# A decoder layer on one core: one sum of magnitudes for two weight pieces, a plain copy of the total, and scaled scores written back to PSUM

## The chip, the core and the metric

The kernel runs on one core of one Trainium2 chip. The core has five engines with queues of their own: TensorE (PE, matrix multiply; PEld is its weight load), VectorE (DVE), ScalarE (ACT), GpSimd (POOL) and SyncE (SP, which here only issues transfers). They meet through semaphores. Matrix products are written to PSUM (eight banks of 128 partitions x 512 fp32 values), everything else lives in SBUF. The metric is the device time of one execution in microseconds, lower is better.

## What is computed

A decoder layer with three residual blocks, each followed by a layer norm: self attention with 16 heads of 128 on x of 2 x 512 x 512, whose weights are 4-bit codes times a scale per 32 rows; cross attention against a memory of 2 x 1024 rows with only the 54 largest scores of a row kept; and a gated feed-forward block.

```python
w = codes * jnp.repeat(scales, 32, axis=0)            # for q, k, v and o
scores = einsum('bqhd,bkhd->bhqk', q, k) / sqrt(128)
attn = softmax(scores, axis=-1)
out = einsum('bhqk,bkhd->bqhd', attn, v)              # then o, residual, layer norm
# cross attention: scores, keep the 54 largest of 1024, softmax, product, W_o, residual, layer norm
# feed forward: silu(x Wg) * (x Wu), then Wd, residual, layer norm
```

The change touches the self attention alone.

## The kernel before, in words

To keep fp32 accuracy on TensorE, every operand is split into a high half (rounded to the format that TensorE reads, written by ACT) and a low half (the remainder, written by DVE or POOL), and a product is the sum of three matmuls: low x high, high x high, high x low. For the four weights the low half is often all zero, since a 4-bit code times a power of two is exact in the high half. The kernel finds that out at run time. For each weight key (a head pair of q and k, a group of v, a pair of o) it sums the magnitudes of the low half, and if the sum is 0 it skips the matmuls with the low half by a branch in `mm_if` (line 105).

That sum is made of these steps. When the low half of a piece (128 x 512) has been written, `check_lo` (line 225) notes it. `run_checks` (line 228) stands near the end of each step of the main loop and takes up to two noted pieces from the list, each with one ACT instruction `Abs` with an accumulated sum into a column of `mag` (line 235). The hardware runs that as two instructions, the ACTIVATE and an ACTIVATION_READ_ACCUMULATOR. A q/k key (18 of them) has two pieces, w = 0 for q and w = 1 for k; an o key (8) has two pieces; a v key (4) has four. When the last piece of a key is summed, `run_sums` (line 241) in the next step adds the 128 partitions with one small matmul against `ones` (line 247), and ACT adds the two or four columns with a copy that accumulates into `flag` (line 250). TensorE's queue later loads the flag (line 109).

The main loop (line 1099) runs over 128 steps i = 4 j + qt, where j is a pair of head and batch and qt a quarter of the rows. Each step puts on the queues, for TensorE in this order: projections of the next j (`proj_qk`, qt 0 and 1), at qt 3 the transposes of step i, at qt 0 the product with V (`av`), at qt 2 and 3 the output projection (`proj_o`), in some j the V projection (`proj_v`), else the transposes, then `scores(i + 2)` (three matmuls), and from `run_sums` the sum of magnitudes. `scores` (line 494) also puts on DVE a multiply by minus the scale with a running minimum (line 503), whose full output goes to a scrap tile `JK` in bf16 and whose minimum goes to `nms`. `softexp(i + 2)` (line 507) is the exponential on ACT, which reads the raw scores in PSUM again, multiplies by the scale `ssc` (one value per partition, from SBUF) for heads above 1 and a constant for heads 0 and 1. All queues are first in, first out, in the order in which the program's steps are written; within a step ACT gets evacuations (L370, L396, L438, L535, L554), the exponential, then the checks, then high halves of new weight pieces (L277). DVE gets the minimum (L503) ahead of the low halves of q/k (L373) and of the transposed probabilities (L538). `run_sums` does nothing at qt = 0.

Where a v key's last piece is noted (step 3 of the j with j % 8 = 5), the first piece of a q/k key is noted in the same step, so `run_checks` takes both in the step after.

Of the kernel before, what the change touches and what calls it, by code (L numbers as in the profile page):

```python
# [63 lines left out]
def decoder_layer(nc, xT, xn, wq, sq, wk, sk, wv, sv, wo, so, bqk, bv, bo,  # L64
                  xwq, xwo, ctxT, ctxn, scal, wg, wu, wd, rq, rk, out):
    with ExitStack() as top:
# [81 lines left out]
        mag = sbt(top, "mag", [128, 4, 4])  # L148
        fsum = sbt(top, "fsum", [1, 4])
        flag = sbt(top, "flag", [1, 32])  # L150
        ssc = sbt(top, "ssc", [128, 2])
        JA = sbt(top, "JA", [128, 512], BF16)
# [27 lines left out]
        JK = sbt(ph1, "JK", [128, 512], BF16)  # L180
# [42 lines left out]
        FL = {}  # L223

        def check_lo(key, lo, tl):
            checks.append((now[0], key, lo, tl))

        def run_checks():
            for _ in range(2):
                if not checks or checks[0][0] >= now[0]:  # L230
                    return
                _, key, lo, tl = checks.pop(0)
                n, col, ts = FL.setdefault(key, (4 if key[0] == "v" else 2, len(FL), []))
                m = mag[:, col % 4, len(ts):len(ts) + 1]
                T[("JA",)] = op(act, lambda e, lo=lo, m=m: e.activation(JA[:, :], lo, ACT.Abs, accum_out=m),  # L235
                                tl, T.get(("JA",)), T.get(("flag", col - 4)))
                ts.append(T[("JA",)])
                if len(ts) == n:
                    sums.append((now[0], key))

        def run_sums():
            while sums and sums[0][0] < now[0]:
                _, key = sums.pop(0)
                n, col, ts = FL[key]
                k, ps = fbank()
                o = ps[0:1, 0:n]
                t = pe.add(lambda e, o=o, col=col, n=n: e.matmul(o, ones[:, 0:1], mag[:, col % 4, 0:n],  # L247
                                                                 start=True, stop=True),
                           flat([ts, t_one, bank[5 + k]]), True)
                t = op(act, lambda e, o=o, col=col, n=n: e.activation(fsum[:, 0:n], o, ACT.Copy,  # L250
                                                                       accum_out=flag[:, col:col + 1]),
                       t, T.get(("flag", col - 1)))
                bank[5 + k] = T[("flag", col)] = t

        def flag_of(key):
            c = FL[key][1]
# [237 lines left out]
        def scores(i):  # L494
# [8 lines left out]
            tm = op(dve, lambda e: e.tensor_scalar(JK[:, :], ps, nsc, None, ALU.mult, ALU.min, accum_out=m),  # L503
# [942 lines left out]
```

How the kernel before makes its waits and increments, by code:

```python
    def emit(self, eng):  # L38
        reached = {}
        for waits, fn, inc in self.items:
            for sem, v in waits:
                if reached.get(id(sem), 0) < v:
                    reached[id(sem)] = v
                    eng.wait_ge(sem, v)
            if fn is None:
                continue
            ins = fn(eng)
            if inc:
                ins.then_inc(self.sem, 1)
# [33 lines left out]
            def load(self, dst, src, *waits, q=sp):  # L83
                self.n += 1
                s = self.sem
                q.add(lambda e: e.dma_start(dst, src).then_inc(s, 16), flat(waits), False)
                return (s, 16 * self.n)
```

## Time and profile before

| what | value |
|---|---|
| median of 3 runs | 970.77 us (970.51 to 971.89) |
| the profiled execution's own time | 969.9 us |
| its span in the trace | 968.0 us |
| instructions in the trace | 13301 |
| TensorE matmul busy | 928.5 us (96%) |
| ACT busy, DVE busy, POOL busy | 580.8, 577.3, 473.7 us |
| self attention (the main loop) | about 27 to 545 us of the span |

Times in the rows are microseconds from the start of the span. "Busy" of TensorE counts a matmul of 512 columns as about 0.39 us, though such matmuls start every 0.23 us when nothing holds them, so a busy TensorE can hide short holes. Where a row ends in brackets, they give the engine's idle time before it and the instruction whose end released it. Self attention, in which all that the change touches lies, is the first 545 us.

### The profile page before, as it was taken

What the parts mean: (1) busy time and instruction counts of PE and PEld (TensorE: products, weight loads), DVE (VectorE), ACT (ScalarE), POOL (GpSimd) and SP (SyncE); (2) the same over time, 40 slices, a digit from 0 to 9 for tenths busy, and PEclk for the clock granted to TensorE, in tenths of its full rate; (3) what the DMA queues carried; (4) which work ended last, traced back from release to release, by engine and by line L of the source; (5) the groups of instructions that cost most, each with busy time, mean ns of one, the idle gap of its engine ahead of it and who ended that gap; (6) DMA issues with size and microseconds to landing.
All of it is one profiled execution on the core that took longest, in us unless ns stands there. A gap on an engine that the chain in (4) does not pass through costs nothing.

```text
span 968.0 us, 13301 instructions
## 1 busy us (share of the span) xinstructions
PE 928.5 (96%) x4516; PEld 751.6 (78%) x4516; DVE 577.3 (60%) x1057; ACT 580.8 (60%) x1201; POOL 473.7 (49%) x375
## 2 busy tenths in 40 slices
PE   9999899999999999999999999899999899999997
PEld 7777678877788777877667777788878788788886
DVE  5676756567566666565675799884878314511114
ACT  5667866678767778687775446443564634443333
POOL 4246642545515356466554347452684652354440
PEclk9999999999999999999999999989999999999999
DMA  6531220212300222222222112331443341243331
GB/s 197 153 109 44 85 85 1 62 54 71 87 12 28 88 58 68 66 60 72 50 66 87 55 55 88 88 98 50 126 110 98 89 141 43 76 134 97 99 87 43
DMA packets 46101, 76.97 MB, mean 80 GB/s; under 512 B 5584, under 2 KB 11216, under 8 KB 45776
## 3 DMA queue, kind: packets, MB, share of 16 engines
q1 hardware_dynamic: 45600, 75.68, 26.8%
q8 instruction: 41, 0.67, 0.3%
q10 hardware_dynamic: 432, 0.39, 0.1%
q14 instruction: 28, 0.23, 0.1%
HBM read 73.69 MB, written 2.36 MB: 79 GB/s over the span
## 4 chain that ended last, share of the span: by engine, by line
PE 81%; DVE 9%; ACT 5%; issue 3%; DMA 1%; POOL 0%; SPq 0%; DVEq 0%; ACTq 0%; POOLq 0%
PE p L99 75%; PE p L528 5%; DVE JK L503 2%; DVE acc L447 1%; ACT PR L511 1%; ACT JA L235 1%; DVE PT L538 1%; DVE QK L373 1%; DMA acc<-in_xT 1%; DVE m L726 1%; PE p L779 1%; DVE st L588 0%; PE p L636 0%; DVE SX L737 0%; PE p L247 0%
## 5 line engine op out<-in xcount | busy, mean ns | idle before, releaser
L503 DVE TENSOR_SCALAR_CACHE_REDUCE JK<-p,ssc 128x512 bf16<-128x512 f32 x112 | 83.8, 748 | 149.5 <-PE p L99 149.1
L654 POOL TENSOR_TENSOR V<-RAW,V 128x512 fp32r<-128x512 f32 x64 | 82.6, 1311 | 141.8 <-ACT V L653 141.7
L444 POOL TENSOR_TENSOR acc<-SX,acc 128x512 f32<-128x512 f32 x52 | 68.7, 1320 | 169.8 <-ACT SX L438 131.4
L99 PE MATMUL p<-R 128*128 128x512 f32 x544 | 136.8, 394 | 2.0 <-DVE V L399 0.8
L99 PE MATMUL p<-QK 128*128 128x512 f32 x384 | 117.4, 414 | 4.5 <-DVE QK L373 4.1
L511 ACT ACTIVATE PR<-p,nms,ssc 128x512 f32<-128x512 f32 x112 | 87.2, 778 | 57.5 <-DVE JK L503 57.1
L99 PEld LDWEIGHTS p<-R 128*128 128x128 f32 x544 | 100.9, 188 | 26.5 <-issue 1.4
L99 PE MATMUL p<-R,V 128*128 128x512 f32 x480 | 113.4, 392 | 0.8 <-ACT C L653 0.8
L99 PEld LDWEIGHTS p<-R,V 128*128 128x128 f32 x480 | 90.6, 189 | 20.1 <-issue 1.2
L275 POOL TENSOR_TENSOR RAW<-RAW,SCL 128x512 f32<-128x512 f32 x65 | 87.4, 1350 | 27.0 <-DMA SCL<-in_so 14.3
L654 POOL TENSOR_TENSOR C<-RAW,C 128x512 fp32r<-128x512 f32 x58 | 75.9, 1322 | 41.1 <-ACT C L653 41.1
L99 PE MATMUL p<-PT,V 128*128 128x512 f32 x384 | 93.6, 393 | 1.9 <-DVE PT L538 1.9
L99 PE MATMUL p<-C 128*128 128x512 f32 x384 | 92.5, 390 | 0.2 <-issue 0.2
L99 PE MATMUL p<-WV,R 128*128 128x512 f32 x368 | 91.0, 394 | 1.3 <-DVE JK L503 1.1
L99 PE MATMUL p<-V 128*128 128x512 f32 (+1 forms) x432 | 90.8, 367 | 0.7 <-POOL V L654 0.7
L887 DVE TENSOR_TENSOR SX<-p,SX 128x512 f32<-128x512 f32 x32 | 22.1, 691 | 115.0 <-PE p L99 108.9
L538 DVE TENSOR_TENSOR PT<-p,PT 128x512 fp32r<-128x512 f32 x128 | 87.4, 683 | 5.0 <-ACT PT L535 4.9
L99 PEld LDWEIGHTS p<-PT,V 128*128 128x128 f32 x384 | 70.6, 188 | 20.4 <-issue 2.5
L99 PEld LDWEIGHTS p<-V 128*128 128x128 f32 x432 | 74.5, 189 | 14.1 <-ACT V L653 1.1
L99 PEld LDWEIGHTS p<-C 128*128 128x128 f32 x384 | 71.7, 188 | 15.2 <-issue 0.6
L99 PEld LDWEIGHTS p<-WV,R 128*128 128x128 f32 x368 | 67.8, 188 | 18.7 <-issue 3.0
L99 PE MATMUL p<-WO,OT 128*128 128x512 f32 x256 | 74.7, 412 | 3.2 <-DVE acc L447 2.7
(170 smaller groups left out, 1665.8 us busy)
## 6 DMA issues: line engine op xcount, KB each, us to landing
RAW<-in_wg SPq DMA_DIRECT2D x32, 256.0 KB, 2.8
RAW<-in_wu SPq DMA_DIRECT2D x32, 256.0 KB, 2.7
RAW<-in_ctxn SPq DMA_DIRECT2D x32, 256.0 KB, 2.8
RAW<-in_wd SPq DMA_DIRECT2D x32, 256.0 KB, 2.8
RAW<-in_wq SPq DMA_DIRECT2D x19, 256.0 KB, 2.7
RAW<-in_wk SPq DMA_DIRECT2D x18, 256.0 KB, 2.7
RAW<-in_wv SPq DMA_DIRECT2D x16, 256.0 KB, 2.8
RAW<-in_wo SPq DMA_DIRECT2D x16, 256.0 KB, 4.4
```

Source lines behind the costliest of these rows:

```text
L99: return e.matmul(outp, a, b, start=st, stop=sp_)
L235: T[("JA",)] = op(act, lambda e, lo=lo, m=m: e.activation(JA[:, :], lo, ACT.Abs, accum_out=m), tl, T.get(("JA",)), T.get(("flag", col - 4)))
L275: tm = op(em, lambda e: e.tensor_tensor(rv, rv, sv_, ALU.mult), td, ts)
L373: tl = op(dve, lambda e: e.scalar_tensor_tensor(out=lo, in0=ps, scalar=bias, in1=hi, op0=ALU.add, op1=ALU.subtract), th, free, T_BQK)
L444: pool, lambda e: e.tensor_tensor(a, buf, a, ALU.add), ts, T[("acc", r)])
L447: bank[5 + k] = T[("scaled", j)] = T[("acc", r)] = op(dve, lambda e: e.scalar_tensor_tensor(out=a, in0=ps, scalar=s, in1=a, op0=ALU.mult, ...
L503: tm = op(dve, lambda e: e.tensor_scalar(JK[:, :], ps, nsc, None, ALU.mult, ALU.min, accum_out=m), T[("S", i)], T.get(("max", i - 1)), T.g ...
L511: T[("exp", i)] = op(act, lambda e: e.activation(PR[:, i % 2, :], ps, ACT.Exp, bias=m, scale=sc, accum_out=rs[:, i % 8:i % 8 + 1]), T[("ma ...
L528: t = pe.add(lambda e, c=c: e.transpose(tp[:, c], PR[:, i % 2, c], ident[:, :]), flat([T[("exp", i)], free, t_id]) if kt == 0 else [], kt ...
L538: tl = op(dve, lambda e: e.tensor_tensor(lo, tv, hi, ALU.subtract), th, fr)
L654: tl = op(pool, lambda e: e.tensor_tensor(lo, raw, hi, ALU.subtract), th, free)
L887: t = op(dve, lambda e: e.tensor_tensor(hf, u, hf, ALU.mult), T[("g", n, 1)], t)
```

## The change

It has three parts.

1. `check_lo` now collects the pieces of a key and notes the key once, when its last piece is written. `run_checks` takes one key in a step and sums two pieces (128 x 2 x 512) with one `Abs`: one instruction for a q/k or o key, two for a v key. In all 34 `Abs` of 1024 elements stand in for 68 of 512.
2. `run_sums` adds the partials of a v key in PSUM (two small matmuls that accumulate), so that one value is left, and ACT writes it to `flag` with a plain copy. The tile `fsum` and the wait for the flag before go.
3. The minimum on DVE writes the scaled scores over the raw ones in PSUM (fp32, 128 x 512) instead of a scrap tile in SBUF (bf16), and the exponential reads them with the constant factor -1 instead of the scale from SBUF. The wait of a minimum for the minimum before goes.

```diff
-        mag = sbt(top, "mag", [128, 4, 4])
-        fsum = sbt(top, "fsum", [1, 4])
+        mag = sbt(top, "mag", [128, 4, 2])
-        JA = sbt(top, "JA", [128, 512], BF16)
+        JA = sbt(top, "JA", [128, 2, 512], BF16)
-        JK = sbt(ph1, "JK", [128, 512], BF16)
...
         def check_lo(key, lo, tl):
-            checks.append((now[0], key, lo, tl))
+            n, ts = PIECES.setdefault(key, (4 if key[0] == "v" else 2, []))
+            ts.append(tl)
+            if len(ts) == n:
+                checks.append((now[0], key, list(ts)))
...
         def run_checks():
-            for _ in range(2):
-                if not checks or checks[0][0] >= now[0]:
-                    return
-                _, key, lo, tl = checks.pop(0)
-                n, col, ts = FL.setdefault(key, (4 if key[0] == "v" else 2, len(FL), []))
-                m = mag[:, col % 4, len(ts):len(ts) + 1]
-                T[("JA",)] = op(act, lambda e, lo=lo, m=m: e.activation(JA[:, :], lo, ACT.Abs, accum_out=m),
-                                tl, T.get(("JA",)), T.get(("flag", col - 4)))
-                ts.append(T[("JA",)])
-                if len(ts) == n:
-                    sums.append((now[0], key))
+            if not checks or checks[0][0] >= now[0]:
+                return
+            _, key, ts = checks.pop(0)
+            col = FL.setdefault(key, len(FL))
+            lo = low_halves(key)
+            done = []
+            for n in range(0, lo.shape[1], 2):
+                m = mag[:, col % 4, n // 2:n // 2 + 1]
+                T[("JA",)] = op(act, lambda e, m=m, n=n: e.activation(JA[:, :, :], lo[:, n:n + 2, :], ACT.Abs, accum_out=m),
+                                ts, T.get(("JA",)), T.get(("flag", col - 4)))
+                done.append(T[("JA",)])
+            sums.append((now[0], key, done))

         def run_sums():
...
-                t = pe.add(lambda e, o=o, col=col, n=n: e.matmul(o, ones[:, 0:1], mag[:, col % 4, 0:n],
-                                                                 start=True, stop=True),
-                           flat([ts, t_one, bank[5 + k]]), True)
-                t = op(act, lambda e, o=o, col=col, n=n: e.activation(fsum[:, 0:n], o, ACT.Copy,
-                                                                       accum_out=flag[:, col:col + 1]),
-                       t, T.get(("flag", col - 1)))
+                for n in range(len(ts)):
+                    t = pe.add(lambda e, ps=ps, col=col, n=n: e.matmul(
+                        ps[0:1, 0:1], ones[:, 0:1], mag[:, col % 4, n:n + 1], start=n == 0, stop=n == len(ts) - 1),
+                        flat([ts, t_one, bank[5 + k]]), n == len(ts) - 1)
+                t = op(act, lambda e, ps=ps, col=col: e.activation(flag[:, col:col + 1], ps[0:1, 0:1], ACT.Copy), t)
...
-            tm = op(dve, lambda e: e.tensor_scalar(JK[:, :], ps, nsc, None, ALU.mult, ALU.min, accum_out=m),
-                    T[("S", i)], T.get(("max", i - 1)), T.get(("exp", i - 4)))
+            tm = op(dve, lambda e: e.tensor_scalar(ps, ps, nsc, None, ALU.mult, ALU.min, accum_out=m),
+                    T[("S", i)], T.get(("exp", i - 4)))
...
-            sc = ssc[:, 0:1] if HB[i // 4][0] > 1 else SC
...
-                PR[:, i % 2, :], ps, ACT.Exp, bias=m, scale=sc, accum_out=rs[:, i % 8:i % 8 + 1]),
+                PR[:, i % 2, :], ps, ACT.Exp, bias=m, scale=-1.0, accum_out=rs[:, i % 8:i % 8 + 1]),
```

## Rows read from the trace of the kernel before

**Rows 1.** The page: busy us, share of the span, instructions, by engine
```profile
PE 928.5 (96%) x4516; PEld 751.6 (78%) x4516; DVE 577.3 (60%) x1057; ACT 580.8 (60%) x1201; POOL 473.7 (49%) x375
```

**Rows 2.** Three stretches: length, busy PE, PEld, DVE, ACT, POOL, TensorE clock, DMA, GB/s
```profile
0.00:545.00 545.00, 528.88 (x2560) 416.40 (x2561) 344.34 (x696) 384.95 (x875) 267.29 (x215) 1.00 0.24 71
...
618.00:628.60 10.60, 7.07 (x35) 5.38 (x33) 8.82 (x16) 4.26 (x8) 2.56 (x2) 1.00 0.18 53
...
628.70:638.90 10.20, 7.40 (x33) 7.03 (x34) 10.13 (x19) 7.70 (x15) 8.24 (x7) 0.50 0.27 77
```

**Rows 3.** Groups by line and shape: busy us, mean ns of one, idle before
```profile
L511 ACT ACTIVATE PR<-p,nms,ssc 128x512 f32<-128x512 f32 x112 | 87.2, 778 | 57.5 <-DVE JK L503 57.1
L503 DVE TENSOR_SCALAR_CACHE_REDUCE JK<-p,ssc 128x512 bf16<-128x512 f32 x112 | 83.8, 748 | 149.5 <-PE p L99 149.1
...
L235 ACT ACTIVATE JA<-R 128x512 bf16<-128x512 f32 x36 | 22.3, 619 | 0.3
...
L602 DVE TENSOR_SCALAR acc<-acc,mv,rstd 128x512 f32<-128x512 f32 x20 | 12.6, 675 | 0.2
...
L511 ACT ACTIVATE PR<-p,nms 128x512 f32<-128x512 f32 x16 | 11.0, 688 | 9.3 <-DVE JK L503 9.3
...
L235 ACT ACTIVATION_READ_ACCUMULATOR JA<-R 128x1 f32 x36 | 6.8, 189 | 0.0
...
L734 ACT ACTIVATE SCL<-SX,nmx 128x1024 f32<-128x1024 f32 x4 | 4.6, 1152 | 0.0
...
L924 DVE TENSOR_TENSOR acc<-p,acc 128x512 f32<-128x512 f32 x4 | 2.7, 680 | 1.1 <-PE p L99 1.1
```

**Rows 4.** Who waited for whom: us in total, times, longest
```profile
PEld p L247 <- ACT JA L235: 8.5, 14, 1.4
...
PE p L99 <- DVE QK L373: 4.4, 15, 0.9
PE p L247 <- ACT JA L235: 3.3, 4, 1.0
```

**Rows 5.** Timeline of a step with a q/k sum: start, length, engine, line
```profile
196.29 0.78 ACT L511 ACTIVATE PR<-p,nms,ssc 128x512 f32<-128x512 f32 x1 [0.42 <-DVE JK L503]
...
197.06 0.62 ACT L235 ACTIVATE JA<-R 128x512 bf16<-128x512 f32 x1
197.06 0.93 PE L99 MATMUL p<-QK 128*128 128x512 f32 x3 [0.25 <-DVE QK L373]
...
197.58 0.19 ACT L235 ACTIVATION_READ_ACCUMULATOR JA<-R 128x1 f32 x1
...
197.93 0.19 PE L247 MATMUL p<-mag,ones 128*1 128x2 f32 x2
```

**Rows 6.** Timeline of a step with a v sum
```profile
249.89 0.62 ACT L235 ACTIVATE JA<-WV 128x512 bf16<-128x512 f32 x1
...
250.41 0.19 ACT L235 ACTIVATION_READ_ACCUMULATOR JA<-WV 128x1 f32 x1
250.69 0.63 ACT L235 ACTIVATE JA<-R 128x512 bf16<-128x512 f32 x1
...
251.20 0.19 PE L247 MATMUL p<-mag,ones 128*1 128x4 f32 x2
```

**Rows 7.** Timeline of the steps around an o sum
```profile
238.10 0.62 ACT L235 ACTIVATE JA<-WO 128x512 bf16<-128x512 f32 x1
...
239.79 0.08 DVE L503 DVE_READ_ACCUMULATOR JK<-p,ssc 128x1 f32 x1
...
240.28 0.78 ACT L511 ACTIVATE PR<-p,nms,ssc 128x512 f32<-128x512 f32 x1
...
241.56 0.21 ACT L235 ACTIVATION_READ_ACCUMULATOR JA<-WO 128x1 f32 x1
...
241.86 0.19 PE L247 MATMUL p<-mag,ones 128*1 128x2 f32 x2 [0.78 <-ACT JA L235]
...
242.24 0.47 PE L99 MATMUL p<-R 128*128 128x512 f32 x1 [0.19 <-issue]
```

More of the change, by code:

```diff
@@ L222, in decoder_layer @@
         checks, sums = [], []
-        FL = {}
+        FL, PIECES = {}, {}
         def check_lo(key, lo, tl):
-            checks.append((now[0], key, lo, tl))
-        def run_checks():
-            for _ in range(2):
-                if not checks or checks[0][0] >= now[0]:
-                    return
-                _, key, lo, tl = checks.pop(0)
-                n, col, ts = FL.setdefault(key, (4 if key[0] == "v" else 2, len(FL), []))
-                m = mag[:, col % 4, len(ts):len(ts) + 1]
-                T[("JA",)] = op(act, lambda e, lo=lo, m=m: e.activation(JA[:, :], lo, ACT.Abs, accum_out=m),
-                                tl, T.get(("JA",)), T.get(("flag", col - 4)))
-                ts.append(T[("JA",)])
-                if len(ts) == n:
-                    sums.append((now[0], key))
+            n, ts = PIECES.setdefault(key, (4 if key[0] == "v" else 2, []))
+            ts.append(tl)
+            if len(ts) == n:
+                checks.append((now[0], key, list(ts)))
@@ new lines, in low_halves @@
+        def low_halves(key):
+            if key[0] == "v":
+                return WV[:, 1, :, :]
+            if key[0] == "o":
+                return WO[:, key[1] % 2, :, 1, :]
+            return WQK[:, key[1] % 2, :, 1].rearrange("p w k c -> p w (k c)")
+        def run_checks():
+            if not checks or checks[0][0] >= now[0]:
[10 more added lines that the diff above has]
+            sums.append((now[0], key, done))
@@ L241, in run_sums @@
         def run_sums():
             while sums and sums[0][0] < now[0]:
-                _, key = sums.pop(0)
-                n, col, ts = FL[key]
+                _, key, ts = sums.pop(0)
+                col = FL[key]
                 k, ps = fbank()
-                o = ps[0:1, 0:n]
-                t = pe.add(lambda e, o=o, col=col, n=n: e.matmul(o, ones[:, 0:1], mag[:, col % 4, 0:n],
-                                                                 start=True, stop=True),
-                           flat([ts, t_one, bank[5 + k]]), True)
@@ L253, in run_sums @@
+                t = op(act, lambda e, ps=ps, col=col: e.activation(flag[:, col:col + 1], ps[0:1, 0:1], ACT.Copy), t)
                 bank[5 + k] = T[("flag", col)] = t
         def flag_of(key):
-            c = FL[key][1]
+            c = FL[key]
             return flag[0:1, c:c + 1].bitcast(I32), T[("flag", c)]
```

## The prediction, made before the result

> **What bounds the kernel now.** I read the page first. TensorE is busy 96% of the span, ACT and DVE 60% each [rows 1]. Over the first 545 us, where all of the change lies, TensorE is busy 528.9 us at the full clock and ACT 385.0 us, that is 71% [rows 2]. So TensorE sets the time, and 16 us of open holes are left in this stage. Work taken off ACT or DVE counts only where TensorE waits for exactly that work, and work that comes later counts in full where TensorE waits for it. The table of waits says who it waits for. The longest entry by far is the small matmul of the sum of magnitudes (L247) waiting for ACT's `Abs`: 8.5 us at the weight load and 3.3 us at the matmul, 18 times. The next is the first scores of a new j, which wait for the low half of q/k on DVE, 15 times, 4.4 us [rows 4]. The change moves both places. It takes instructions off ACT and makes the last one before each sum longer. The third view is the timeline around the 30 sums, for the slack between the end of the accumulator read and the sum on TensorE. There are four kinds:
>
> - **Tight q/k sums.** At 197.93 the sum starts 0.16 us after the read ends at 197.58 + 0.19 [rows 5]. Ten sums look like this one: at 72.6, 86.3, 197.9, 211.5, 322.4, 335.9, 447.8, 461.4, 477.4 and 492.0 us, the first two with a slack of 0.25.
> - **Sums that stall already.** At 241.86 TensorE stood idle 0.78 us and started 0.09 us after the read's end at 241.56 + 0.21 [rows 7]. So 0.09 is the gap when the sum waits for the read. Four of these, all for o, at 117.4, 241.9, 366.4 and 464.8.
> - **v sums** with four columns. At 251.20 the v read ended at 250.60, 0.60 us before [rows 6]. Three of these, at 126.7, 251.2 and 375.7. The first v sum at 35.2 is apart.
> - The other twelve have 0.7 to 2.9 us of slack.
>
> **The long `Abs`.** The trace has no `Abs` of 1024. A 128x512 takes 619 ns, and the read behind it 189. An exponential of 1024 takes 1152 with a bias from SBUF; a factor from SBUF costs ACT 778 - 688 = 90 ns in L511 [rows 3]. Taking 90 off for the bias gives 1.06 us, so the second half costs 0.43 us (1.06 - 0.62). Bounds: 0.37 (1.152 against the dearest exponential of 512, 0.778) and 0.53 (1.152 - 0.619, nothing taken off). An `Abs` of 512 takes 0.80 from start to start [rows 6], so one of 1024 takes 1.23. ACT loses 34 x (0.80 - 0.43) = 13 us of work, the 30 accumulator reads after the flag copy another 5.6 us at 0.19, and 112 exponentials 90 ns each, 10 us [rows 3]. That is 28 us of ACT in all, and it lies beside TensorE's work except as follows.
>
> **What it does to each kind.** A q/k key's two `Abs` ran in two consecutive steps, right behind the exponential. Now the first is gone and the second is 0.43 longer, and the sum is still in the step behind. The exponential before it starts when DVE's minimum is done (it waits 0.42 us for it [rows 5]), so taking the first `Abs` away does not start it earlier. Only its own 0.09 is gained. The read ends 0.34 later, of which 0.07 is slack (0.16 - 0.09), so the sum waits 0.27 us and TensorE with it. I count nine of the ten (2.4 us); the one at 461.4 is followed 3.4 us later by a stalled o sum that takes it up.
>
> For the stalled o sums the first `Abs`, at 238.10, is removed, and ACT runs without a pause from there to the exponential at 240.28. That one can come earlier until the minimum, which ended at 239.87, holds it: by some 0.36. With its own 0.09 the `Abs` starts 0.45 earlier and lasts 0.43 longer [rows 7]. Four times nothing.
>
> A v key's four `Abs` were spread over four steps, and only the last, with a q/k `Abs` behind it, stood before the sum. Now both long ones do. The first starts at 249.80, the second 1.23 later at 251.03, its read starts 0.95 on (0.52 plus 0.43) and ends at 252.17; with 0.09 the sum starts at 252.26 instead of 251.20, 1.06 later [rows 6]. Three times, 3.2 us. ACT's next evacuations move by about the same, no more than TensorE does. The q/k `Abs` moves to the step behind, where its sum had 2.8 us of slack. The first v sum: both long `Abs` now run in a stretch where ACT waits until 30 us anyway, and a plain copy brings the flag some 0.1 us sooner, which is waited for: -0.1.
>
> Where a sum stalls, TensorE's queue has drained, and what its sequencer does next is exposed. After the stalled sum the next matmul starts 0.38 us on (242.24), after the sum at 197.93 another starts 0.12 on [rows 5, 7]. The difference is the load of a flag, which follows each v sum too: 3 x 0.26 = 0.8 us. A tight q/k sum is followed by transposes with no load: 0, at most 9 x 0.26 = 2.3. The extra small matmul of a v key adds 0.03 us.
>
> **The scores written back.** DVE writes no PSUM in this trace. Its operations of 512 elements that differ in where they read take 675 ns (SBUF) and 680 (PSUM), and the largest step between forms of the minimum is 748 against that 675, 73 ns [rows 3]. I take 0 for the price, with bounds of -30 and +75 ns. The minimum stands on the path at the first scores of a new j, 15 times, since DVE's low half is queued behind it [rows 4], and at some ten places late in the stage; so -0.7 to +1.9 us. The dropped wait for the minimum before is on the same queue and long met. The constant factor is worth 90 ns of the exponential, already counted.
>
> The Trainium skill (Perfetto Trace Analysis, Optimizing Scalar/DVE Operations) gives DVE about 60 ns per access on SBUF and 125 on PSUM. By that the minimum would take 65 ns more and the sum 1.6 us more; the rows of reads do not show such a difference.
>
> **The sum.** 2.4 + 3.2 + 0.8 - 0.1 = +6.3 us on the profiled execution's 969.9, so 976.2. The median of the runs lies 0.9 above that execution, so 977.1 us.
>
> **The rivals.**
>
> - **Faster: the relief of ACT removes the stalls.** If ACT is generally late rather than at the last `Abs`, 28 us less work pulls the exponential and the read ahead, the four stalled o sums lose their 0.78 and 0.26 us, and half of the 4.4 us at first scores goes too. 970.8 - 4.2 - 2.2 = 964.4 us. For it: the exponential at 240.28 was late by 0.36 us. Against: in [rows 5] it waited for DVE. It decides from the point where an `Abs` of 1024 costs under 0.1 us more than one of 512. Chance 0.15. The same page and section says that larger operations improve throughput "if the engine is saturated", and that where ACT causes bubbles on others though it isn't, "breaking up instructions may allow work to be completed sooner". ACT at 71% with TensorE waiting for it is that second case, which agrees with my forecast.
> - **No change: what the sums lose is given back.** Later waits of TensorE on DVE could shrink when TensorE comes later. They are waits behind a minimum that itself follows TensorE's scores, so I give it little: 970.8 + 0.8 = 971.6 us, chance 0.15.
> - **Slower still: the write to PSUM is slow.** If DVE paid a second pass over the elements (0.53 us, as the 512 elements take), 25 places would cost 13 us: 990 us, chance 0.05. If it only pays the 75 ns and sequencer time is exposed at each q/k sum, 977.1 + 1.9 + 2.3 = 981.3, which is inside my range.
> - **The clock.** TensorE ran at half clock (1.2 of 2.4 GHz) from 628.7 to 638.9 us, after a stretch of 10.6 us in which it was busy for 7.1 [rows 2]. The change moves this by 6 us. If the slow stretch fell away, at most 5 us come back (972); if such a one were added, 982. Chance 0.1 in all, one half each.
> - **The change does not do what it says** on the factor: if the constant -1 gained nothing, each sum would wait 0.09 longer, 1.1 us in all. The 16 exponentials with a constant speak against it [rows 3]. It stays in the range.
>
> **How the numbers follow.** The forecast of 977.1 has 0.55, with a range of its own of 974 to 981 (the long `Abs` at 0.37 to 0.53 acts once in nine sums and twice in three, so -0.9 and +1.5, DVE by -0.7 and +1.9). A range of 80% reaches over the clock's and the no-change case down to 970, and up to 981.5. A measurement of this kernel can tell about 0.2% (1.9 us) from no change. Faster by more: 0.15. Within 0.2%: the no-change case and a little of the rest, 0.17. Slower: 0.68.
>
> **What would show it.** `Abs` x34 at 1.04 to 1.06 us. The wait of L247 for ACT's `Abs` grows from 11.8 us to 17 or more and from 18 times to over 28. The ten tight sums show a gap of 0.09 instead of 0.16, the v sums start about 1.1 us later behind their scores. The minimum stays near 748 ns, the exponential falls to 688. I would be wrong if the waits at L247 shrink, if the minimum's row moves by more than 75 ns, or if the waits for L373 change by more than 2 us.

## The result and the profile after

The changed kernel takes 977.83 us (median of 4 runs, 977.24 to 978.35), the kernel before 970.64 (4 runs, 969.92 to 971.89). The ratio is 1.0068 with an interval of 1.0057 to 1.0080, so the change costs 7 us. The forecast was 977.1.

| what | before | after |
|---|---|---|
| profiled execution, its span | 969.9, 968.0 us | 977.64, 975.8 us |
| instructions in the trace | 13301 | 13072 |
| ACT busy | 580.8 us | 562.9 us |
| TensorE waits for ACT's `Abs` at the sum (at the weight load + at the matmul; the two overlap in time) | 8.5 + 3.3 us | 15.6 + 8.0 us |
| main loop, first transpose of `PR` to last | 512.2 us | 519.2 us |

The last row is the measure that the rest of this text uses. The loop's start differs by 1.4 us between two profiles of the changed kernel (31.6 and 30.2), and the stages behind the loop, which no edit touches, take 425.0 to 428.2 us in the thirteen profiles of this text. So one span says little about an edit of 1 us, and the loop more. It is read from the view of one tile: operation, lengths, start of the first and of the last. Before:

```profile
L528 PE MATMUL p<-ident,PR x512: 270/272/330, 30.0 to 542.2; 128*128 128x128 f32 x171
```

After:

```profile
L534 PE MATMUL p<-ident,PR x512: 270/272/330, 31.6 to 550.8; 128*128 128x128 f32 x171
```

The loop is 7.0 us longer with 18 us less work on ACT. The engines' line of the page after answers to [rows 1]:

```profile
PE 930.0 (95%) x4524; PEld 751.1 (77%) x4524; DVE 578.6 (59%) x1057; ACT 562.9 (58%) x1103; POOL 473.1 (48%) x375
```

Two stretches of after, with the columns of [rows 2]: the self attention, and the 10 us in which TensorE is granted half its clock, which came 7 us later with everything else.

```profile
0.00:553.60 553.60, 531.79 (x2568) 416.76 (x2569) 346.03 (x696) 367.17 (x777) 267.05 (x215) 1.00 0.24 70
...
635.80:646.00 10.20, 6.05 (x28) 5.69 (x29) 10.09 (x20) 8.36 (x15) 6.90 (x6) 0.51 0.23 60
```

The groups by line and shape, against [rows 3]:

```profile
L517 ACT ACTIVATE PR<-p,nms 128x512 f32<-128x512 f32 x128 | 87.8, 686 | 80.6 <-DVE p L510 80.4
L510 DVE TENSOR_SCALAR_CACHE_REDUCE p<-p,ssc 128x512 f32<-128x512 f32 x112 | 84.7, 756 | 150.3 <-PE p L99 150.3
...
L245 ACT ACTIVATE JA<-R 128x1024 bf16<-128x1024 f32 x18 | 18.8, 1046 | 0.0
...
L510 DVE DVE_READ_ACCUMULATOR p<-p,ssc 128x1 f32 x112 | 15.8, 141 | 0.0
...
L256 PE MATMUL p<-mag,ones 128*1 128x1 f32 x68 | 5.9, 164 | 8.0 <-ACT JA L245 8.0
```

The long `Abs` takes 1046 ns, the exponential 686, the minimum 756 (748 before). The group of the accumulator read behind the minimum was not among the rows of before; there it was

```profile
L503 DVE DVE_READ_ACCUMULATOR JK<-p,ssc 128x1 f32 x112 | 9.2, 82 | 0.0
```

so writing fp32 to PSUM instead of bf16 to SBUF costs this second instruction 59 ns, and the first only 8.

The waits of after, against [rows 4], twice as long at the sum (15.6 + 8.0 against 11.8 us) and hardly moved at the first scores:

```profile
PEld p L256 <- ACT JA L245: 15.6, 18, 1.5
...
PE p L256 <- ACT JA L245: 8.0, 17, 1.1
PE p L99 <- DVE QK L380: 4.8, 17, 0.9
```

A tight q/k sum of after in the timeline, the one of [rows 5]. The read ends at 201.91 and the sum starts 0.05 later, with TensorE idle for 0.22. From the start of the scores (three matmuls) to the sum it is 1.15 us (201.96 - 200.81), where it was 0.87 (197.93 - 197.06 [rows 5]):

```profile
200.77 1.05 ACT L245 ACTIVATE JA<-R 128x1024 bf16<-128x1024 f32 x1
200.81 0.94 PE L99 MATMUL p<-QK 128*128 128x512 f32 x3 [0.25 <-DVE QK L380]
201.72 0.19 ACT L245 ACTIVATION_READ_ACCUMULATOR JA<-R 128x1 f32 x1
...
201.96 0.19 PE L256 MATMUL p<-mag,ones 128*1 128x1 f32 x2 [0.22 <-ACT JA L245]
```

The v step of [rows 6]. Both long `Abs` stand ahead of the sum, which waits 1.05 us, has four instructions instead of two, and is followed by a longer group of bias matmuls. From the start of the scores to the sum it is 1.99 us (256.70 - 254.71):

```profile
254.24 1.05 ACT L245 ACTIVATE JA<-WV 128x1024 bf16<-128x1024 f32 x1
...
254.71 0.94 PE L99 MATMUL p<-QK 128*128 128x512 f32 x3
...
255.41 1.06 ACT L245 ACTIVATE JA<-WV 128x1024 bf16<-128x1024 f32 x1
256.37 0.19 ACT L245 ACTIVATION_READ_ACCUMULATOR JA<-WV 128x1 f32 x1
256.70 0.24 PE L256 MATMUL p<-mag,ones 128*1 128x1 f32 x4 [1.05 <-ACT JA L245]
256.87 1.62 PE L99 MATMUL p<-WO,bv_r 128*2 128x512 f32 x4
```

Before, the scores of the same step, 0.88 us ahead of the sum at 251.20, and the bias matmuls right behind it:

```profile
250.32 0.95 PE L99 MATMUL p<-QK 128*128 128x512 f32 x3
...
251.32 1.22 PE L99 MATMUL p<-WO,bv_r 128*2 128x512 f32 x4
```

The o step of [rows 7], where the sum waits 0.76 us instead of 0.78:

```profile
244.30 0.69 ACT L517 ACTIVATE PR<-p,nms 128x512 f32<-128x512 f32 x1 [0.22 <-DVE p L510]
244.98 1.05 ACT L245 ACTIVATE JA<-WO 128x1024 bf16<-128x1024 f32 x1
245.93 0.19 ACT L245 ACTIVATION_READ_ACCUMULATOR JA<-WO 128x1 f32 x1
246.17 0.19 PE L256 MATMUL p<-mag,ones 128*1 128x1 f32 x2 [0.76 <-ACT JA L245]
```

### The profile page after: what moved, and what is told of

Its sections match the earlier page's. It is cut to its first block, busy times and chain, and to the rows that moved or that the text cites. A ratio compares the mean times of both kernels' runs of the same rounds, so it can differ in the third digit from the quotient of the medians.

```text
span 975.8 us, 13072 instructions
## 1 busy us (share of the span) xinstructions
PE 930.0 (95%) x4524; PEld 751.1 (77%) x4524; DVE 578.6 (59%) x1057; ACT 562.9 (58%) x1103; POOL 473.1 (48%) x375
## 4 chain that ended last, share of the span: by engine, by line
PE 80%; DVE 10%; ACT 5%; issue 3%; POOL 1%; DMA 1%; SPq 0%; ACTq 0%; DVEq 0%; POOLq 0%
PE p L99 74%; PE p L534 5%; DVE p L510 2%; ACT JA L245 2%; DVE acc L454 2%; DVE PT L544 1%; DMA acc<-in_xT 1%; DVE QK L380 1%; ACT PR L517 1%; PE p L785 1%; DVE st L594 0%; DVE m L732 0%; DVE WV L288 0%; PE p L256 0%; ACT SG L625 0%
## 5 line engine op out<-in xcount | busy, mean ns | idle before, releaser
L510 DVE TENSOR_SCALAR_CACHE_REDUCE p<-p,ssc 128x512 f32<-128x512 f32 x112 | 84.7, 756 | 150.3 <-PE p L99 150.3
L517 ACT ACTIVATE PR<-p,nms 128x512 f32<-128x512 f32 x128 | 87.8, 686 | 80.6 <-DVE p L510 80.4
L544 DVE TENSOR_TENSOR PT<-p,PT 128x512 fp32r<-128x512 f32 x128 | 87.4, 683 | 6.9 <-ACT PT L541 4.2
L534 PE MATMUL p<-ident,PR 128*128 128x128 f32 x512 | 77.7, 274 | 0.0
```

Source lines behind the costliest of these rows:

```text
L510: tm = op(dve, lambda e: e.tensor_scalar(ps, ps, nsc, None, ALU.mult, ALU.min, accum_out=m), T[("S", i)], T.get(("exp", i - 4)))
L517: T[("exp", i)] = op(act, lambda e: e.activation(PR[:, i % 2, :], ps, ACT.Exp, bias=m, scale=-1.0, accum_out=rs[:, i % 8:i % 8 + 1]), T[(" ...
L534: t = pe.add(lambda e, c=c: e.transpose(tp[:, c], PR[:, i % 2, c], ident[:, :]), flat([T[("exp", i)], free, t_id]) if kt == 0 else [], kt ...
L544: tl = op(dve, lambda e: e.tensor_tensor(lo, tv, hi, ALU.subtract), th, fr)
```

## The experiments

The theory after the result was that of the forecast: the loss is the length of the last `Abs` before each sum, q/k sums losing 0.3 us and v sums over 1 us each, with parts 2 and 3 worth nothing. The expectations call it theory A. The rivals were that the write to PSUM costs something, and that the relief of ACT is worth something which the sums hide. All runs together, each ratio against the kernel before in runs on the same chip:

| run | what it is | median us | ratio (95%) | loop us |
|---|---|---|---|---|
| p1_checks_only | part 1 alone | 979.94 | 1.0095 (1.0078 to 1.0111) | 520.6 |
| p2_copy_only | part 2 alone | 971.80 | 1.0007 (0.9998 to 1.0015) | 513.6 |
| p3_scores_only | part 3 alone | 970.70 | 0.9994 (0.9980 to 1.0008) | 511.7 |
| p1_and_p3 | the change without part 2 | 978.98 | 1.0070 (1.0054 to 1.0085) | 520.4 |
| after_again | the changed kernel again | 977.77 | 1.0058 (1.0045 to 1.0071) | 520.6 |
| v_pairs | the change, v summed in two steps | 975.24 | 1.0047 (1.0031 to 1.0064) | 516.5 |
| late_sums | without part 2, q/k and o sums a step later | 1004.27 | 1.034 (1.032 to 1.036) | 548.0 |
| checks_first | the change, `Abs` ahead of the exponential | 970.09 | 0.9986 (0.9976 to 0.9995) | 510.4 |
| checks_first_v_pairs | both of these | 968.79 | 0.9974 (0.9965 to 0.9984) | 509.7 |
| before_checks_first | the kernel before, `Abs` ahead | 967.60 | 0.9962 (0.9948 to 0.9975) | 508.8 |
| before_checks_first_p3 | the same with part 3 | 967.20 | 0.9954 (0.9941 to 0.9967) | 508.4 |

Against a loop of 512.2 us before and 519.2 after. The loops of p1_checks_only, p1_and_p3 and after_again each contain a stretch of 3.4 us at half clock, on which the last section has more; late_sums has five of them and the others none. One place moves a loop by up to 0.7 us beside what an edit is about: the product with V at about 62 us, which waits for `PT` (0.4 to 0.5 us in v_pairs, p2_copy_only and checks_first, 0.1 in the changed kernel, not at all in the kernel before). Why was not followed up, so a difference of under 0.7 us between two loops is no finding.

### Part 1 alone

The kernel before with the long `Abs` and one note for each key. The wider `JA` left no room in SBUF for `JK`, so the minimum's scrap output went into the part of `PR` that the exponential of the same step writes afterwards, with the waits that this needs.

```diff
-        JA = sbt(top, "JA", [128, 512], BF16)
-        JK = sbt(ph1, "JK", [128, 512], BF16)
+        JA = sbt(top, "JA", [128, 2, 512], BF16)
...
+            JK = PR[:, i % 2, 0:256].bitcast(BF16)
             tm = op(dve, lambda e: e.tensor_scalar(JK[:, :], ps, nsc, None, ALU.mult, ALU.min, accum_out=m),
-                    T[("S", i)], T.get(("max", i - 1)), T.get(("exp", i - 4)))
+                    T[("S", i)], T.get(("T", i - 2)), T.get(("exp", i - 2)), T.get(("exp", i - 4)))
```

> The kernel before with part 1 alone (one Abs for two pieces). The partials are added as before, with the accumulating copy; the minimum writes its bf16 scrap into the half of PR that the exponential overwrites next (SBUF has no room for JK beside the wider JA), and the exponential reads the raw scores with its scale from SBUF. Theory A (the long Abs ahead of its sum is the whole loss): as slow as the changed kernel or up to 1.5 us slower, since the exponential keeps its 90 ns: 978 to 979.5 us. Rival B (the write back to PSUM and the longer accumulator read of the minimum behind it are the loss): 970.6 us, as before.

The ratio is 1.0095, and TensorE waits at the sum as it does in the changed kernel:

```profile
PEld p L258 <- ACT JA L246: 16.2, 18, 1.5
...
PE p L258 <- ACT JA L246: 8.5, 17, 1.1
```

Part 1 alone costs all that the change costs. The loop is 520.6 us, and 519 or so without its half-clock stretch, by what such a stretch cost the changed kernel (520.6 against 519.2). The median is 0.4 us above what was expected and 2 us above the changed kernel's. What makes these 2 us is not told apart: this kernel also lacks part 3 and has the moved scrap tile.

### Part 3 alone

```diff
-            tm = op(dve, lambda e: e.tensor_scalar(JK[:, :], ps, nsc, None, ALU.mult, ALU.min, accum_out=m),
-                    T[("S", i)], T.get(("max", i - 1)), T.get(("exp", i - 4)))
+            tm = op(dve, lambda e: e.tensor_scalar(ps, ps, nsc, None, ALU.mult, ALU.min, accum_out=m),
+                    T[("S", i)], T.get(("exp", i - 4)))
...
-                PR[:, i % 2, :], ps, ACT.Exp, bias=m, scale=sc, accum_out=rs[:, i % 8:i % 8 + 1]),
+                PR[:, i % 2, :], ps, ACT.Exp, bias=m, scale=-1.0, accum_out=rs[:, i % 8:i % 8 + 1]),
```

> The kernel before with part 3 alone (scaled scores written to PSUM, constant factor -1). Theory A: within 0.7 us of before, rather below, since four sums that wait gain 0.09 us each: 969.5 to 970.8 us. Rival B: 974 us or more.

0.9994 with 1 in the interval, and the waits at the sum 1 us shorter than before (10.8 against 11.8):

```profile
PEld p L247 <- ACT JA L235: 8.0, 14, 1.2
...
PE p L247 <- ACT JA L235: 2.8, 4, 0.8
```

The write to PSUM costs nothing that the time shows. The step of [rows 5] in this kernel's timeline tells why the 90 ns that the exponential saves don't arrive in full either:

```profile
195.53 0.76 DVE L503 TENSOR_SCALAR_CACHE_REDUCE p<-p,ssc 128x512 f32<-128x512 f32 x1 [0.35 <-PE p L99]
196.21 0.14 DVE L503 DVE_READ_ACCUMULATOR p<-p,ssc 128x1 f32 x1
196.21 0.75 DVE L373 SCALAR_TENSOR_TENSOR QK<-p,bqk_t,QK 128x512 fp32r<-128x512 f32 x1
...
196.38 0.69 ACT L510 ACTIVATE PR<-p,nms 128x512 f32<-128x512 f32 x1 [0.51 <-DVE p L503]
...
197.06 0.62 ACT L235 ACTIVATE JA<-R 128x512 bf16<-128x512 f32 x1
```

In the kernel before, the minimum of this step was

```profile
195.49 0.75 DVE L503 TENSOR_SCALAR_CACHE_REDUCE JK<-p,ssc 128x512 bf16<-128x512 f32 x1 [0.35 <-PE p L99]
```

The exponential starts 0.85 us after the minimum starts (196.38 - 195.53). Before it was 0.80 (196.29 [rows 5] less 195.49). The `Abs` starts 1.53 after the minimum instead of 1.57. So where the exponential waits for the minimum, part 3 gains 0.04 us, since the longer accumulator read takes the other 0.05.

### Part 2 alone, and the change without it

```diff
-                t = pe.add(lambda e, o=o, col=col, n=n: e.matmul(o, ones[:, 0:1], mag[:, col % 4, 0:n],
-                                                                 start=True, stop=True),
...
+                for c in range(n):
+                    t = pe.add(lambda e, ps=ps, col=col, c=c, n=n: e.matmul(
+                        ps[0:1, 0:1], ones[:, 0:1], mag[:, col % 4, c:c + 1], start=c == 0, stop=c == n - 1),
...
-                t = op(act, lambda e, o=o, col=col, n=n: e.activation(fsum[:, 0:n], o, ACT.Copy,
-                                                                       accum_out=flag[:, col:col + 1]),
-                       t, T.get(("flag", col - 1)))
+                t = op(act, lambda e, ps=ps, col=col: e.activation(flag[:, col:col + 1], ps[0:1, 0:1], ACT.Copy), t)
```

> The kernel before with part 2 alone: the two or four partials added by as many small matmuls that accumulate in PSUM, and the plain copy to the flag. Theory A: each further small matmul costs TensorE some 0.05 to 0.07 us (26 ns between the two halves of one, up to 0.07 between two), 26 keys with one more and 4 with three more, so 2 to 2.7 us more, less 0.1 for the sooner flag: 972.5 to 973.5 us. Rival: nothing, 970.6, since the weight load of a single column hides.

The loop is 1.4 us longer, the ratio 1.0007 with 1 just inside. With the short `Abs` there are two columns for a q/k or o key and four for v, so this kernel adds 38 small matmuls (26 + 4 x 3) where the change adds four (one for each v key). The median of 971.80 lies between what theory A expected (972.5 to 973.5) and the rival's 970.6, so theory A put the extra matmuls too high. Of the 1.4 us, 0.7 come at the product with V at 62 us. Each further small matmul puts 0.05 us between the sum and the next matmul (0.17 us from start to start instead of 0.12), and only a part of that stays in the loop. The change has four of them and not 38. The other way round, the changed kernel with the accumulating copy:

```diff
-                for n in range(len(ts)):
-                    t = pe.add(lambda e, ps=ps, col=col, n=n: e.matmul(
-                        ps[0:1, 0:1], ones[:, 0:1], mag[:, col % 4, n:n + 1], start=n == 0, stop=n == len(ts) - 1),
...
+                t = pe.add(lambda e, o=o, col=col, n=n: e.matmul(o, ones[:, 0:1], mag[:, col % 4, 0:n],
+                                                                 start=True, stop=True),
...
-                t = op(act, lambda e, ps=ps, col=col: e.activation(flag[:, col:col + 1], ps[0:1, 0:1], ACT.Copy), t)
+                t = op(act, lambda e, o=o, col=col, n=n: e.activation(fsum[:, 0:n], o, ACT.Copy,
+                                                                       accum_out=flag[:, col:col + 1]),
+                       t, T.get(("flag", col - 1)))
```

> The changed kernel without part 2: the partials of a key as columns of one small matmul and the accumulating copy, as before. Theory A with the price of part 2 as its run alone showed it (0.6 to 1.4 us): here only the four v keys have a second column, so 4 x 0.07 us less and nothing else: 977 to 978 us. If part 2 costs by the copy and not by the matmuls, 976.5 us or less.

1.0070 against the 1.0058 of the changed kernel beside it: the intervals overlap, and the loops, both with one half-clock stretch, are 520.4 and 520.6 us. The median of 978.98 is 1 us above what was expected, and its runs spread from 976.26 to 980.96, so neither price of part 2 is confirmed; it is too small to be seen here. The plain copy saves ACT 30 reads of 0.19 us that nobody on the path waited for.

### The changed kernel again

> The changed kernel once more, beside the others on the same chip, for its loop from the first transpose to the last: 519.2 us in its first trace, against 512.2 before. Theory A: 519 to 519.5 again, and 977 to 978.5 us in all, with the difference to the trace before it in the start or the second stage.

977.77 us, as in the first runs, with a loop of 520.6, where 519 to 519.5 had been expected. It is 1.4 us over the first profile's loop, and the last section shows the stretch that differs.

### v summed as its pieces come

The changed kernel, with a v key noted twice, after its second and its fourth piece, so that one long `Abs` goes into each of two steps.

```diff
-            if len(ts) == n:
-                checks.append((now[0], key, list(ts)))
+            if len(ts) % 2 == 0:
+                checks.append((now[0], key, ts[-2:], len(ts) - 2, len(ts) == (4 if key[0] == "v" else 2)))
...
-            for n in range(0, lo.shape[1], 2):
-                m = mag[:, col % 4, n // 2:n // 2 + 1]
-                T[("JA",)] = op(act, lambda e, m=m, n=n: e.activation(JA[:, :, :], lo[:, n:n + 2, :], ACT.Abs, accum_out=m),
-                                ts, T.get(("JA",)), T.get(("flag", col - 4)))
-                done.append(T[("JA",)])
-            sums.append((now[0], key, done))
+            m = mag[:, col % 4, n // 2:n // 2 + 1]
+            T[("JA",)] = op(act, lambda e, m=m, n=n: e.activation(JA[:, :, :], lo[:, n:n + 2, :], ACT.Abs, accum_out=m),
+                            ts, T.get(("JA",)), T.get(("flag", col - 4)))
+            DONE.setdefault(key, []).append(T[("JA",)])
+            if last:
+                sums.append((now[0], key, DONE[key]))
```

> The changed kernel, but a v key's first two pieces are summed by their Abs of 1024 as soon as they are written, one step earlier work, so that one long Abs and not two stands before the v sum. Theory A: the three v sums no longer wait, and their 1.1 us each with the flag loads exposed behind them goes: 4 to 5 us less than the changed kernel, 972.9 to 973.8 us. Rival C (TensorE's wait at the v sums is made up later, the loss is elsewhere): 977 to 978 us.

975.24 us, 2.6 below the changed kernel, and the expectation is missed by 1.4. The v sums no longer wait. The waits; then the first scores of a new j, 13 us ahead of a v sum, and that v sum:

```profile
PEld p L257 <- ACT JA L245: 12.3, 18, 1.2
...
PE p L257 <- ACT JA L245: 4.8, 14, 0.7
```

```profile
240.40 0.93 PE L99 MATMUL p<-QK 128*128 128x512 f32 x3 [0.40 <-DVE QK L381]
...
253.72 0.24 PE L257 MATMUL p<-mag,ones 128*1 128x1 f32 x4
253.90 1.47 PE L99 MATMUL p<-WO,bv_r 128*2 128x512 f32 x4
```

The wait at the matmul fell by 3.2 us, as the three 1.05 of the v sums say. The loop gave back 2.7 (519.2 - 516.5). The sum keeps its four instructions (0.24 us against 0.19), and the bias matmuls behind it stay longer than before (1.47 against 1.22), though nothing is waited for. The loop is still 4.3 us over that of before. Set side by side transpose by transpose, the two traces show where. About 2.0 are the q/k sums and 0.6 the product with V at 62 us. Around each v sum the loop loses 0.2 to 0.4 more, of which the two rows explain 0.3, and in the two steps around the o sum ahead of it another 0.4, 1.2 us in all three. There the first long `Abs` of the v key now stands (at 237.24, 1.04 us long) ahead of ACT's high half of q/k. DVE's low half then starts 0.15 us later against the minimum's read, and the first scores wait 0.40 us for it instead of 0.25. The expectation had taken this `Abs` for free.

### The sums a step later

If the `Abs` is late by 0.3 us, the sum could stand one step later on TensorE's queue. The copy is the one before the change, since the order of flags changes.

```diff
-            while sums and sums[0][0] < now[0]:
+            while sums and sums[0][0] < now[0] - (0 if sums[0][1][0] == "v" or sums[0][1] == ("o", 7) else 1):
```

> The changed kernel with the sums of q/k and o keys put on TensorE's queue one step later (v sums and the last o sum stay; the copy of the total is the accumulating one of before, since the order of the flags changes). Theory A: the ten tight sums and the four that stalled already no longer wait: 2.9 + 4 us less, 970.5 to 971.5 us. Rival C: the waits only move to the next place where TensorE depends on ACT: 976 us or more.

1004.27 us, 33 us over the kernel before, where a time like that kernel's was expected. At these sums TensorE no longer waits for `Abs` but for the flag, which the very next projection loads:

```profile
PE p L99 <- ACT fsum L261: 15.7, 12, 2.6
```

```profile
209.46 0.19 PE L258 MATMUL p<-mag,ones 128*1 128x1 f32 x2
...
210.61 0.14 ACT L261 ACTIVATE fsum<-p 1x1 f32<-1x1 f32 x1
...
211.24 0.94 PE L99 MATMUL p<-R 128*128 128x512 f32 x3 [1.58 <-ACT fsum L261]
```

The sum runs at 209.46, its copy comes to ACT's turn 1.15 us later, and the projection starts at 211.24. In the order of before TensorE had other work in that time: behind the sum at 197.93 its copy ran at 198.72, during transposes, the output projection and scores. The sum's place is bounded from both sides, by the `Abs` ahead of it and by the flag behind it. The loop is 28.8 us longer than the changed kernel's, and this wait is 15.7 us. TensorE also waits more for the minimum (L514, 9.9 us in 12 places) and for `PT` (L548, 7.4 in 8, against 1.8 in 4 of after), and the five half-clock stretches come on top. These entries overlap and were not divided further.

### The `Abs` ahead of the exponential

In most steps ACT's exponential waits for DVE's minimum (80.4 us in all in the group of L517 above), and the `Abs` stands behind it. Its data is there a step earlier. So it can fill that wait, and its place, not its length, would decide. The edit, in the changed kernel:

```diff
+            run_checks()
             if i + 2 < 4 * NJ:
                 softexp(i + 2)
-            run_checks()
```

> The changed kernel with one edit: in each step the Abs are put on ACT's queue ahead of the exponential instead of behind it, so that they run while ACT waits for the minimum (0.42 us in a tight q/k step, 0.85 in a v step). No instruction is added or taken away. Theory A (what counts is how late the last Abs ends against its sum): the ten tight sums lose their 0.29 us, the v sums their 1.1, and of the four o sums' 0.8 and 0.26 most goes: 9 to 10 us less than the changed kernel, 967 to 969 us, below the kernel before. Rival D (the exponential, now 1.3 to 2.3 us later in those steps, becomes what TensorE waits for, by way of the transposes or the scores two steps on): 975 us or more.

970.09 us, 7.7 below the changed kernel (9 to 10 were expected, so it is 1.1 above the expected range), and by the table of waits and the timeline the wait at the sum is all but gone:

```profile
PEld p L256 <- ACT JA L245: 1.1, 3, 0.4
```

```profile
195.49 1.06 ACT L245 ACTIVATE JA<-R 128x1024 bf16<-128x1024 f32 x1
...
196.24 0.14 DVE L510 DVE_READ_ACCUMULATOR p<-p,ssc 128x1 f32 x1
196.43 0.20 ACT L245 ACTIVATION_READ_ACCUMULATOR JA<-R 128x1 f32 x1
196.53 0.69 ACT L517 ACTIVATE PR<-p,nms 128x512 f32<-128x512 f32 x1
...
198.00 0.19 PE L256 MATMUL p<-mag,ones 128*1 128x1 f32 x2
```

The `Abs` starts while the minimum is still running on DVE, its read ends at 196.63, and the sum at 198.00 has 1.4 us of slack. The exponential starts 0.15 us after the minimum's read ended, no longer at once. That is the price, and it shows downstream: TensorE's waits for `PT` (L544) are 3.6 us in 7 places, against 1.8 in 4 of after. Three of them, 0.6 us each, stand at the product with V behind an o sum (at 119.9, 244.0 and 368.1), where after has none, and one is that at 62 us.

With v in two steps as well (the two diffs above together):

> The same, and a v key summed in two halves as its pieces come. Theory A: the v sums wait for nothing already with the edit before, so within 1 us of it. Rival D: clearly faster than the edit before, since the exponential behind two long Abs in a row is then held up by one only.

968.79 us, 1.3 below, where within 1 was expected. The loops are 0.7 apart and the intervals of the two ratios overlap, so that v in two steps adds something here is not shown. Then the same order in the kernel before, with its short `Abs`:

```diff
+            run_checks()
             if i + 2 < 4 * NJ:
                 softexp(i + 2)
-            run_checks()
```

> The kernel before with the same order, Abs ahead of the exponential. It keeps the 68 short Abs. Theory A: only the four o sums waited in it, 0.8 us and 0.26 each, so 3 to 4 us less than before: 967 to 968 us, and no slower than the changed kernel with this order by more than 1 us. If the relief of ACT by the change is worth something by itself (rival E), the changed kernel with this order is faster than this one by more than 2 us.

967.60 us, 0.9962. This speaks against the rival of ACT's relief. With the sums' waits all but gone from both, the kernel with 18 us less work on ACT is the slower one, by 2.5 us in the median (the intervals of the ratios don't touch) and by 1.6 in the loop (510.4 against 508.8). Of these 1.6, 0.7 are the product with V at 62 us and 0.9 the three behind the o sums, which here wait 0.3 us each and not 0.6: the long `Abs` holds the exponential up longer than a short one does. A gain by the relief that is smaller than this loss is not excluded. Before the move, ACT idled 57.5 us ahead of L511 [rows 3]; now

```profile
L511 ACT ACTIVATE PR<-p,nms,ssc 128x512 f32<-128x512 f32 x112 | 87.1, 778 | 41.9 <-DVE JK L503 40.4
```

so 15.6 us of the `Abs` went into a wait that was there anyway. Part 3 on top of it (the two diffs of this kernel and of part 3 together):

> The kernel before with the Abs ahead of the exponential, and with part 3 (scaled scores to PSUM, constant factor). Where no sum waits for ACT any more, 90 ns off an exponential lie beside TensorE's work: within 1 us of the same order without part 3, 966.5 to 968 us. If the shorter exponential is worth something on TensorE's path (rival E), 965.5 us or less.

967.20 us, 0.9954 (0.9941 to 0.9967), with the shortest loop of all (508.4). It beats both kernels, by 4.3 us the one before (971.46 beside it) and by 10.6 the changed one. That part 3 has a share in it is not shown: the intervals of the last two ratios overlap for the most part, and the loops are 0.4 us apart.

## Why the prediction was right, point by point

**The bound.** TensorE waits for exactly the last `Abs` before a sum. Part 1 alone brings the whole loss, and moving the `Abs` takes it away.

**Tight q/k sums.** 0.27 each was forecast. Measured is 0.28 to 0.29, at all ten: in the row at 201.96 it is 1.15 us from the scores to the sum instead of 0.87. Two small errors cancelled. The sum starts 0.05 us after the read's end, not 0.09, so the slack was 0.11 (0.16 - 0.05) and not 0.07. And the `Abs` starts only 0.04 earlier, not 0.09, since the exponential waits for a longer accumulator read. By these 0.43 - 0.04 - 0.11 = 0.28. The first two have 0.25 us of slack and lose as much, for a reason that the forecast doesn't give: their heads had the constant factor before, so they get the dearer accumulator read and no shorter exponential. The step that the o sum behind the one at 461.4 takes its loss up held, and more than that: TensorE's idle time before that o sum fell from 0.98 to 0.39 us, which takes up two q/k losses. And what the last one at 492.0 loses is given back 0.3 us later, where the output projection waits 0.19 us for DVE's `acc` instead of 0.46. Ten times 0.285 less 0.6 and 0.3 is 2.0 us, against the 2.4 forecast.

**Stalled o sums.** Nothing was forecast and 0.76 instead of 0.78 us of idle time measured. The exponential was indeed held by the minimum, 0.22 us in the row at 244.30. The fourth, at 464.8, is the one named above.

**v sums.** This term was mis-sized. The sum was put 1.06 us later and comes 1.11 later (1.99 - 0.88 from the scores), with TensorE idle for 1.05. What was put at 0.26 + 0.01 for each, the exposed load of a flag and the extra small matmul, is 0.45: the bias matmuls take 1.62 us instead of 1.22 and the sum 0.24 instead of 0.19. With the 1.11 that is 1.56 for this one. The lag of the transposes behind those of before grows by 1.5, 1.55 and 1.7 us over the three, 4.7 in all, where 3.2 + 0.8 had been put. With the 2.0 us of the q/k sums and 0.2 at the product with V at 62 us, for which the forecast has no term, it makes 6.9 of the 7.0 us by which the loop grew. So the total came closer than its terms: the v sums are 0.7 dearer, the q/k sums 0.4 cheaper. The comparison with v in two steps says that part of the longer bias group is not tied to the stall at all, as 0.25 of its 0.40 us stayed without it. The forecast had no term for that, and what it is stays open.

**The scores written back.** 0 was taken, within -30 to +75 ns. The minimum costs 8 ns more and its read 59, 67 in all, near the dear end. But the read is not in the way of DVE's next operation: in part 3 alone L373 starts at 196.21, with the read and not behind it. So the first scores wait 4.8 us in 17 places instead of 4.4 in 15, and the interval of part 3 alone contains 1. The range was right and its reason too coarse: the price goes to whoever reads the minimum, not to DVE.

The Trainium skill (Perfetto Trace Analysis, Optimizing Scalar/DVE Operations) has DVE pay some 65 ns more for an access on PSUM than on SBUF. The trace agrees only in the sum of the two instructions, 67 ns, and not in its place: 59 of them are in the accumulator read.

**The relief of ACT.** 28 us less work was forecast and 17.9 came (580.8 - 562.9). The forecast took 0.80 us from start to start for a short `Abs`, from two that follow each other directly. With another instruction behind it the next starts 0.61 us on (197.06 to 197.67), and behind a long one 1.04 (200.77 to 201.81), so a pair saves 0.18 us and not 0.37. The read behind a flag copy likewise holds ACT up for 0.10 us and not 0.19. No term of the forecast time rests on this, since in the v step two `Abs` do follow each other directly; only the rival of the relief was made larger by it.

**The sign.** The rival of ACT's relief needed an `Abs` of 1024 at under 0.1 us over one of 512, and it costs 0.43 (1046 - 619 ns). Its second half, that less work on ACT would shorten other waits, is not borne out by the two kernels with the `Abs` ahead. Of what the sums lost, 0.9 us was given back later: 0.6 at the o sum that the forecast had named and 0.3 behind the last q/k sum.

The Trainium skill (Perfetto Trace Analysis, Optimizing Scalar/DVE Operations) says of a ScalarE that isn't saturated but causes bubbles on other engines that "breaking up instructions may allow work to be completed sooner". The trace agrees: joining them, in part 1 alone, cost 0.95% (1.0095).

**The clock.** The forecast gave 0.05 to one more stretch at half clock, for 5 us. In the loop of the first profile there is none, and that of the second has one, which costs 1.4 us.

**Where the time is against the forecast.** The forecast's own range, 974 to 981 us, is a little wider than its terms make it (975.5 to 980.5). 976.2 was forecast for the profiled execution and 977.64 came. The loop's 7.0 us are 0.7 over the 6.3 forecast; the rest is the loop's later start (1.6 us, where two profiles of one kernel differ by 1.4), with 0.8 us back behind the loop.

**The places to look.** `Abs` x34 at 1.05, the exponential at 686 ns, a wait of 23.6 us where 17 or more had been said, and in 18 and 17 places at the weight load and the matmul. These 23.6 us are 11.8 more than before and the loop only 7.0, since the waits at the weight load and at the matmul of one sum are added though they overlap, and the weight load sits idle while a matmul still runs: the longest wait at the weight load is 1.5 us, and at the matmul 1.1. The tight sums show a gap of 0.05 us behind the read where 0.09 had been said.

## What to carry to other kernels

Joining two instructions saves a fixed part on their engine, but pushes the end of the last one back by what the data of the first adds to it (here 0.43 us); before joining, read the slack between that end and its consumer, not the engine's share. If an instruction whose data is long there stands behind one that waits for another engine, move it ahead: here that cost one line and gave 0.4%, where joining lost 0.7%. Before moving a consumer later instead, look at who waits for its result.

## What the runs showed of the chip that was not expected

**Where and how the minimum is written shows in its accumulator read.** DVE's minimum over 512 values takes 748 ns with a bf16 output in SBUF and 756 with an fp32 output in place in PSUM, and the accumulator read behind it 82 and 141 ns. Width and place changed together, so which of them it is stays open.

**TensorE at half clock for 3.4 us, in some executions and not in others.** In the second profile of the changed kernel the granted clock falls from 1.00 to 0.54 (2.4 to 1.2 GHz for nearly all of the stretch) right behind the v sum's stall. The rows are length, busy time and instructions of PE, PEld, DVE, ACT and POOL, granted clock, DMA share and GB/s:

```profile
126.00:130.00 4.00, 2.87 (x17) 1.49 (x15) 2.98 (x7) 3.97 (x10) 0.00 (x0) 1.00 0.43 139
130.50:133.90 3.40, 3.40 (x9) 2.65 (x9) 1.48 (x3) 1.58 (x3) 0.60 (x1) 0.54 0.11 40
```

The same place in the first profile of the same kernel, by the start of the v sum (128.74 above, 130.08 here):

```profile
127.34:131.34 4.00, 2.85 (x17) 1.48 (x15) 2.97 (x7) 3.97 (x10) 0.00 (x0) 1.00 0.47 137
131.84:135.24 3.40, 3.40 (x18) 2.59 (x17) 1.48 (x3) 1.74 (x4) 1.28 (x2) 1.00 0.11 42
```

TensorE was as busy ahead of it there (2.85 of 4.00 us against 2.87) and kept its clock, with 18 matmuls in the next 3.4 us instead of 9. It cost that loop 1.4 us (520.6 against 519.2). Part 1 alone and the change without part 2 had one such stretch each as well, from 257.9 and from 384.4 us, each again behind the 1 us stall of a v sum. In the loops of the eight kernels whose v sums don't wait there is none. So a stall of 1 us can cost more than itself, but what makes the difference between one execution and the next was not found.
